# Attention blocks on one core: values products on raw fp32, and the block output built with tokens on partitions

## What is computed

```python
xn  = layernorm(x)
# attention branch on xn (it normalizes again)
uv  = silu(layernorm(xn, ln_w, ln_b) @ uv_w.T + uv_b)        # 640 wide
u, v, base = uv[..., :256], uv[..., 256:512], uv[..., 512:]
q, k = rope(base * gamma + beta)
kernel = square(relu(q @ k.T / sqrt(128) + bias))            # 512 x 512 per block
attn = (u * (kernel @ v)) @ o_w.T + o_b + xn
# feed-forward branch on xn
ffn  = squared_relu(xn @ W_sh_up) @ W_sh_down                # shared expert
ffn += sum over the 2 chosen of 8 experts: weight * squared_relu(xn @ W_up[e]) @ W_down[e]
out  = x + attn + ffn
```

## Time and profile before

| what | value |
|---|---|
| runs | 454.51, 454.58, 455.42 us; median 454.58 us |
| the profiled execution, its own time | 456.13 us |
| its span, first to last instruction | 454.3 us |
| mean granted TensorE clock over the span | 0.927 of full |
| busy share of the span | PE 82%, PEld 66%, DVE 65%, ACT 54%, POOL 39% |
| preparation | 0 to 73.9 us |
| turns, from the first rotate_sum to the last mix | 73.9 to 270.3 us |
| expert stage and collection | 271.4 to 454.3 us |

### The profile page before, as it was taken

The page is one execution under the profiler, slowest core; times in us unless marked ns, Lnnn a source line. Parts: engine busy times, 40 slices in busy tenths (PEclk is TensorE's granted clock), DMA queues, the critical chain, the costliest instruction groups (busy, mean ns, idle before and its releaser), DMA issues.

```text
span 454.3 us, 8228 instructions
## 1 busy us (share of the span) xinstructions
PE 371.5 (82%) x2041; PEld 299.2 (66%) x2042; DVE 294.0 (65%) x726; ACT 245.2 (54%) x453; POOL 176.2 (39%) x159
## 2 busy tenths in 40 slices
PE   1168457799998989899999969999999999999800
PEld 1157435566665667566756638999999999999700
DVE  2889798988988888989899822333333333333245
ACT  0203027565676766665656715666666666666400
POOL 0486004562534526180716200444444444444500
PEclk9995567999999999999999997999999999999955
DMA  8618993000000001010100101221222212212089
GB/s 227 212 46 237 231 191 61 29 30 19 23 23 18 29 6 41 0 47 0 41 6 30 42 0 30 66 63 60 64 59 63 64 57 65 64 57 65 36 251 309
DMA packets 49792, 33.65 MB, mean 74 GB/s; under 512 B 5747, under 2 KB 46195, under 8 KB 49780
## 3 DMA queue, kind: packets, MB, share of 16 engines
q1 hardware_dynamic: 29120, 16.27, 12.8%
q10 hardware_dynamic: 16308, 8.26, 9.1%
q0 software_dynamic: 4352, 8.99, 5.5%
HBM read 17.63 MB, written 15.87 MB: 74 GB/s over the span
## 4 chain that ended last, share of the span: by engine, by line
PE 50%; DVE 21%; issue 12%; ACT 6%; ACTq 4%; DMA 4%; DVEq 2%; POOL 0%; POOLq 0%
PE bank L1133 14%; PE bank L1114 7%; PE bank L908 7%; PE bank L909 6%; PE bank L910 6%; DVE work L748 3%; PE bank L1020 3%; ACT base_qk L414 3%; DVE xs L613 3%; ACTq L356 2%; PE bank L946 2%; PE bank L1107 2%; DMA work<-results 2%; DVE qk_lo L725 2%; DVE k_lo L757 2%
## 5 line engine op out<-in xcount | busy, mean ns | idle before, releaser
L865 POOL DMA_INDIRECT slots_in<-xs,slot_now x64 | 75.2, 1176 | 124.5 <-DVE xs L634 77.9
L895 POOL DMA_INDIRECT results<-work x72 | 69.2, 960 | 109.2 <-DVE work L822 107.4
L822 DVE TENSOR_SCALAR work<-bank,work 128x128 f32<-128x128 f32 x72 | 25.2, 350 | 93.5 <-PE bank L1133 93.5
L1133 PEld LDWEIGHTS bank<-wdn,work 128*128 128x128 f32 x576 | 75.1, 191 | 6.0
L1133 PE MATMUL bank<-wdn,work 128*128 x576 | 75.7, 274 | 0.0
L499 ACT ACTIVATE work<-bank 128x512 f32<-128x512 f32 x72 | 43.1, 599 | 14.7 <-PE bank L1114 14.7
L505 ACT ACTIVATE work<-bank 128x512 f32<-128x512 f32 x72 | 43.1, 598 | 8.9 <-PE bank L910 3.4
L1114 PE MATMUL bank<-cst,work 128*128 128x128 f32 x288 | 43.9, 276 | 0.0
L908 PE MATMUL bank<-wup_lo,x_hi 128*128 x72 | 35.3, 491 | 1.0 <-DVE x_lo L813 1.0
L493 ACT CAST x_hi<-bank 128x128 fp32r<-128x128 f32 x72 | 19.0, 266 | 30.8 <-PE bank L1107 30.8
L1114 PEld LDWEIGHTS bank<-cst,work 128*128 128x128 f32 x288 | 34.2, 143 | 0.5 <-issue 0.4
(11 more groups left out here) (177 smaller groups left out, 824.1 us busy)
## 6 DMA issues: line engine op xcount, KB each, us to landing
slots_in<-spare ACTq DMA_DIRECT2D x1, 4680.0 KB, 31.7
work<-slots_in SPq DMA_DIRECT2D x36, 130.0 KB, 2.2
x_all<-in_L_attn_x SPq DMA_DIRECT2D x4, 512.0 KB, 8.7
work<-in_L_ffn_W_up SPq DMA_DIRECT2D x4, 512.0 KB, 3.5
wdn<-in_L_ffn_W_down SPq DMA_DIRECT2D x4, 512.0 KB, 7.3
work<-results SPq DMA_DIRECT2D x8, 256.0 KB, 7.2
work<-results ACTq DMA_DIRECT2D x8, 256.0 KB, 7.7
out<-x_all SPq DMA_DIRECT2D x8, 256.0 KB, 5.7
```

The costliest lines, as they stand in the source:

```text
L865: pool.indirect_dma_start(slots_in, bass.IndirectOffsetOnAxis(slot_now[:, k, t:t + 1], 0), xs1[:, k, t, :], None).then_inc(tokens_sent, 16)
L895: pool.indirect_dma_start(results, bass.IndirectOffsetOnAxis(dest[:, at:at + 1], 0), slot_y[:, k, :], None).then_inc(returned[k], 16)
L1133: last = pe.matmul(P_Y[h][:, 0:D], hid_t[:, h, rows], wdn[:, of, c, :].rearrange("p a d -> p (a d)"), start=(c == 0), stop=(c == HC - 1))
```

## The change

- values: v and kern stay in plain fp32 (v is 128x4x256, kern 128x4x512, all four key tiles at once). No v_split, no kernel_hi, no kernel_lo, one silu of v in place of two. Each `product` of three matmuls becomes one plain fp32 matmul.
- output: the sums in P_OUT have tokens on partitions. The stationary operand is a 128-column slice of sh or g, the moving one shdn or ow with 128 columns; each old matmul becomes four. output_out and output_turned are gone, and mix reads P_OUT. The bias o_b comes in as the first product of the bank: a constant 1/64 stationary (`halves`) times `ob_pair`, which holds o_b rounded to fp32r on 64 partitions and the remainder on the other 64. Two VectorE operations of the preparation build `ob_pair`; o_b is now loaded as a broadcast row.
- order: on TensorE the output of the block before moves behind shared_up 3, shared_down 0 and 1 move behind the base parts, the x1 rows behind values 2. On VectorE mix moves ahead of second_rows_lo. sh has four buffers.

```diff
 act.  def v_silu(b):
-                    act.activation(v_hi[:, 2 * n:2 * n + 2, :]..., part, ACT.Silu)
-                    act.activation(part, part, ACT.Silu).then_inc(v_hi_made, 1)
+                    act.activation(v[:, 2 * n:2 * n + 2, :]..., part, ACT.Silu).then_inc(v_made, 1)
 act.  def turn(b, first, last):
...
-                if not first:
-                    output_out(b - 1)
-                kernel_hi(b, 0)
-                kernel_hi(b, 1)
...
-                kernel_hi(b, 2)
-                kernel_hi(b, 3)
 dve.  preparation, between lnb_bc and uvw_hi
+            dve.memset(halves[:, :].bitcast(F32), 1.0 / HALF)
+            link(prep_chain, dve.tensor_copy(ob_pair[:, :, :], ob_bc[:, :].unsqueeze(1).broadcast_to([P, TB, D])))
+            dve.tensor_tensor(ob_pair[HALF:S], ob_bc[HALF:S, :].unsqueeze(1).broadcast_to([HALF, TB, D]),
+                              ob_pair[HALF:S].bitcast(F32), ALU.subtract).then_inc(ob_made, 1)
 dve.  def turn(b, first, last):
                 kernel_square(b, 0)
                 kernel_square(b, 1)
-                v_split(b)
                 if not last:
                     second_norm(b + 1)
-                kernel_lo(b, 0)
-                kernel_lo(b, 1)
                 kernel_square(b, 2)
                 kernel_square(b, 3)
+                if not first:
+                    mix(b - 1)
                 if not last:
                     second_rows_lo(b + 1)
                     first_norm(b + 1)
-                if not first:
-                    mix(b - 1)
-                kernel_lo(b, 2)
-                kernel_lo(b, 3)
 dve.  def mix(b):
-                dve.wait_ge(out_turned, START + b + 1)
+                dve.wait_ge(out_acc, START + b + 1)
...
-                dve.tensor_tensor(rows, P_FIN[:, :]..., rows, ALU.add).then_inc(mixed, 1)
+                dve.tensor_tensor(rows, P_OUT[:, :]..., rows, ALU.add).then_inc(mixed, 1)
 pe.
+            def output_bias(b):
+                pe.wait_ge(mixed, START + b)
+                pe.matmul(P_OUT[:, :], halves[:, :], ob_pair[:, :, :].rearrange("p t d -> p (t d)"), start=True, stop=False)
+
             def shared_down(b, c):
                 pe.wait_ge(sh_made, START + b * HC + (c + 1))
-                pe.matmul(P_OUT[:, :], shdn[:, c, :], sh[:, c % 2, :], start=(c == 0), stop=False).then_inc(shdn_done, 1)
+                for t in range(TB):
+                    rows = slice(t * P, (t + 1) * P)
+                    last = pe.matmul(P_OUT[:, rows], sh[:, c, rows], shdn[:, c, :], start=False, stop=False)
+                last.then_inc(shdn_done, 1)
...
             def values(b, j):
-                pe.wait_ge(k_lo_made, b * TB + (j + 1))
+                pe.wait_ge(kern_made, b * TB + (j + 1))
...
-                    last = product(P_AV[e][:, :], v_hi[:, j, e * P:(e + 1) * P], v_lo[:, j, e * P:(e + 1) * P],
-                                   k_hi[:, j % 2, :], k_lo[:, j % 2, :], start=(j == 0), stop=(j == TB - 1))
+                    last = pe.matmul(P_AV[e][:, :], v[:, j, e * P:(e + 1) * P], kern[:, j, :], start=(j == 0), stop=(j == TB - 1))
...
             def output(b):
...
-                    last = pe.matmul(P_OUT[:, :], ow[:, e * D:(e + 1) * D], g[:, e, :], start=False, stop=(e == 1))
+                    for t in range(TB):
+                        rows = slice(t * P, (t + 1) * P)
+                        last = pe.matmul(P_OUT[:, rows], g[:, e, rows], ow[:, e * D:(e + 1) * D], start=False, stop=(e == 1 and t == TB - 1))
 pe.   def turn(b, first, last):
                 scores(b, 0)
                 scores(b, 1)
-                if not first:
-                    output(b - 1)
                 scores(b, 2)
                 scores(b, 3)
                 shared_up(b, 2)
                 shared_up(b, 3)
-                pe.wait_ge(out_t_made, START + b)
-                shared_down(b, 0)
-                shared_down(b, 1)
                 if not first:
-                    output_turned(b - 1)
+                    output(b - 1)
                 values(b, 0)
                 if not last:
                     second_rows_turned(b + 1)
                 values(b, 1)
                 if not last:
                     base_part(b + 1)
+                output_bias(b)
+                shared_down(b, 0)
+                shared_down(b, 1)
+                values(b, 2)
+                if not last:
                     first_rows_turned(b + 1)
-                values(b, 2)
                 values(b, 3)
                 shared_down(b, 2)
                 shared_down(b, 3)
```

More of the change, by code:

```diff
@@ L99, in build @@
         x1_hi, x1_lo = sb("x1_hi", [P, T], F32R), sb("x1_lo", [P, T], F32R)
-        v_hi, v_lo = sb("v_hi", [P, TB, EU], F32R), sb("v_lo", [P, TB, EU], F32R)
+        v = sb("v", [P, TB, EU])
         qk_hi, qk_lo = sb("qk_hi", [P, 2, T], F32R), sb("qk_lo", [P, 2, T], F32R)
-        k_hi, k_lo = sb("k_hi", [P, 2, T], F32R), sb("k_lo", [P, 2, T], F32R)
         g = sb("g", [P, 2, T])
+        kern = sb("kern", [P, TB, T])
         cos_sin = sb("cos_sin", [P, 2, T])
@@ L138, in build @@
         rot1, rot2 = cut(3072, (2, T)), cut(4096, (2, T))
-        kern = cut(5120, (2, T))
-        sh = cut(6144, (2, T))
-        out_t = cut(7168, (T,))
         slot_x = cut(0, (2, 2, ROW_W))
@@ L154, in build @@
         inv1, var2, inv2 = sb("inv1", [P, NT]), sb("var2", [P, NT]), sb("inv2", [P, NT])
-        lnw_c, lnb_c, ob_c = sb("lnw_c", [P, 1]), sb("lnb_c", [P, 1]), sb("ob_c", [P, 1])
+        lnw_c, lnb_c = sb("lnw_c", [P, 1]), sb("lnb_c", [P, 1])
+        ob_bc, ob_pair = sb("ob_bc", [P, D]), sb("ob_pair", [P, TB, D], F32R)
+        halves = sb("halves", [P, P], F32R)
+        sh = sb("sh", [P, HC, T])
         uvb_c, uvbias = sb("uvb_c", [P, 4]), sb("uvbias", [P, 4])
@@ L350, in _ @@
         def _(act):
-            for s in (base_made, out_t_made, sh_relu, sh_made, silu_b_made, ut_made):
+            for s in (base_made, sh_relu, sh_made, silu_b_made, ut_made, v_made):
                 act.sem_inc(s, START)
@@ L432, in shared_relu @@
                 product = of_ring(f"sh{c}", b)
-                act.wait_ge(shdn_done, START + b * HC + (c - 1) if c >= 2 else START + b * HC)
-                act.activation(sh[:, c % 2, :], product, ACT.Relu).then_inc(sh_relu, 1)
+                act.wait_ge(shdn_done, START + b * HC)
+                act.activation(sh[:, c, :], product, ACT.Relu).then_inc(sh_relu, 1)
             def shared_square(b, c):
                 act.wait_ge(sh_relu, START + b * HC + (c + 1))
-                act.activation(sh[:, c % 2, :], sh[:, c % 2, :], ACT.Square).then_inc(sh_made, 1)
-            def kernel_hi(b, j):
-                act.wait_ge(kern_made, b * TB + (j + 1))
-                act.wait_ge(av_done, START + b * TB + (j - 1) if j >= 2 else START + b * TB)
-                act.copy(k_hi[:, j % 2, :], kern[:, j % 2, :]).then_inc(k_hi_made, 1)
-            def output_out(b):
-                act.wait_ge(out_acc, START + b + 1)
-                act.wait_ge(out_turned, START + b)
-                act.activation(out_t, P_OUT[:, :], ACT.Identity, bias=ob_c[:, :]).then_inc(out_t_made, 1)
+                act.activation(sh[:, c, :], sh[:, c, :], ACT.Square).then_inc(sh_made, 1)
             def turn(b, first, last):
@@ L482, in _ @@
             sequence_turns(act, turn)
-            output_out(B - 1)
             act.wait_ge(mixed, START + B)
@@ L516, in _ @@
         def _(dve):
-            for s in (rx_copied, qk_made, qk_lo_made, mixed, g_made, kern_biased, x2_lo_made, x1_lo_made, v_biased, v_lo_made, rot2_made):
+            for s in (rx_copied, qk_made, qk_lo_made, mixed, g_made, kern_biased, x2_lo_made, x1_lo_made, v_biased, rot2_made):
                 dve.sem_inc(s, START)
@@ L732, in v_bias @@
                                       vb_bc[:, :].unsqueeze(1).broadcast_to([P, 2, EU]), ALU.add).then_inc(v_biased, 1)
[L734 to L740 removed]
             def kernel_square(b, j):
                 dve.wait_ge(ring_ready, START + b * NRING + (RING.index(f"qk{j}") + 1))
[L745 to L746 removed]
+                if j == 0:
+                    dve.wait_ge(av_done, START + b * TB)
                 at = (TB - 1 - j) * P
[L748 removed]
+                dve.scalar_tensor_tensor(kern[:, j, :], ring(f"qk{j}")[:, :], float(S) ** -0.5,
                                          bias_t[:, at:at + T], ALU.mult, ALU.add).then_inc(kern_biased, 1)
                 dve.wait_ge(kern_biased, START + b * TB + (j + 1))
[L751 removed]
+                dve.scalar_tensor_tensor(kern[:, j, :], kern[:, j, :], 0.0, kern[:, j, :],
                                          ALU.max, ALU.mult).then_inc(kern_made, 1)
[L754 to L758 removed]
             def gate(b):
@@ L902, in _ @@
         def _(pe):
-            for s in (logits_made, rx_turned, shdn_done, av_done, out_acc, out_turned, ring_ready):
+            for s in (logits_made, rx_turned, shdn_done, av_done, out_acc, ring_ready):
                 pe.sem_inc(s, START)
@@ L959, in _ @@
```

(2 more changed lines are left out.)

49 lines of the change are left out of this document (12 added, 37 removed).

## The result

The changed kernel took 471.44 us (median of 472.19, 470.69, 473.5 and 466.0) against 454.58: ratio 1.033, interval 1.024 to 1.042, slower. The ratio is that of the means without 473.5, which lies more than 1.5% above the fastest run of its kernel; all later ratios are made so. The prediction was 443.5 with a range of 440.5 to 449.5. The same file was run again later, unedited, in two other sessions, and took 443.32 us (ratio 0.976, 0.969 to 0.984) and 444.56 us (0.978, 0.971 to 0.984).

What follows compares the result with a forecast made beforehand. VectorE was taken as the bound, TensorE 2.4 us a turn behind. Terms -8.2 - 3.9 + 1.5 - 1.2 + 0.7 = -11.1 us from the profiled 456.13 gave 445.0, or 443.5 against the median; range 440.5 to 449.5.

Steps and rivals of the forecast that it cites:

- Does anything stop TensorE?: Step checking TensorE's handovers through a turn; found four slacks of 0.2 to 0.9 us and a turn of 23.3 us.
- The slower rival: Shared_down and output: loads of 128-column records show, 3.8 us more a turn, 472.7 us in all; chance 0.06.
- the rule of the Trainium skill that the prediction set against its rows: Shared_down and output: loads overlap only for another row group, so 48 records pay 107 ns each, a turn 28.3 us.
- Preparation +0.7: Preparation: two ob_pair operations on VectorE delay uvw_lo by some 1.2 us, partly absorbed; +0.7 us, bounds 0 and 1.4.
- Turn 0, -3.9: First turn, without output: gate comes at 19.3 us in place of 23.25, so -3.9 us.
- Six inner turns, 23.3 each and -8.2: Inner turns: TensorE becomes the bound at 23.3 us a turn in place of 24.67, -8.2 us over six.
- The sum of 23.2: TensorE's work in an inner turn: 22.2 + 1.05 + 0.15 - 0.48 + 0.24 = 23.2 us.
- the 0.1 for add_rows: Inner turns: GpSimd's add_rows stretches a VectorE square, taken as 0.1 us a turn, bound 1.0.
- Last turn +1.5: Last turn, gate to gate: all TensorE at 21.1 us in place of 19.6, +1.5 us.
- Tail -1.2: From the last gate to mix's end: 4.3 us in place of 5.5, as output_out and transposes go, -1.2 us.
- a new wait on TensorE: Rival in the turns: late add_rows or x2_lo takes most of the gain, 24.1 us a turn, 449.1 us; chance 0.17.
- Its SBUF sentence: Squares beside add_rows: by the skill's rule a square that starts first loses nothing, by the rows 1.47 us.

Runs made afterwards that it cites:

- g1: The changed kernel itself, unedited, run again on chip D: 443.32 us, ratio 0.976.
- h1: The changed kernel itself, unedited, run again on chip C: 444.56 us, ratio 0.978.
- f1: The changed kernel with GpSimd's sends of a turn started only when v_bias has read v0: 441.63 us, ratio 0.970.

## Why the prediction was right and wrong

**Against the recorded result it was wrong by 28 us, on the other side.** The step that failed is "Does anything stop TensorE?". It counted each handover from the end of the record, as the trace of before lets one do (0.01 us to the increment), and gave v_part, shared_up and u0 no slack of their own: v_bias was taken as always in time. In the recorded session the word of v0 came 4 us late, and the list of four slacks had no entry for it. The fast session's rows give that slack: v_bias has freed u0's bank at 122.50, and u0 starts at 123.65, 1.15 us later. A v_bias 3.92 us late leaves 2.77, and TensorE stands 2.75. The slower rival came out near the number (472.7 for 471.4) and is wrong all the same: it priced loads that show in the 128-column records, and these run at 0.111 us each in both sessions (sixteen records in 1.95 us, the last one modelled 0.28). By the rule of the Trainium skill that the prediction set against its rows ("TensorE: Matmul & The Clock Gate"; it stands in section "The mechanism", one heading above the one that the prediction names) they would pay a load each; both traces of after disagree with it, as that of before did. The same section also lets a load for the background weight buffer go ahead of running matmuls, and that would fit these rows.

**Against the kernel where its signals come in time it was right, 443.3 and 444.6 for 443.5, and by errors that cancel, so part of it is luck.** By its own steps, from the trace of g1 (span 440.5):

- Preparation +0.7: rotate_sum of turn 0 starts at 74.55 against 73.89, +0.66. Right.
- Turn 0, -3.9: measured 96.45 - 74.55 = 21.90 against 23.25, -1.35. Wrong by 2.5, and by 4.2 in h1, where the turn takes 23.59. I let first_norm alone wait for add_rows in turn 0. The rows show add_rows on the squares, and TensorE, which has no output in this turn, already there:
```profile
83.62 2.31 DVE L726 SCALAR_TENSOR_TENSOR kern<-kern 128x512 f32<-128x512 f32 x1
84.19 1.19 POOL L836 TENSOR_TENSOR x_all<-x_all,xs 128x512 f32<-128x512 f32 x1
85.85 0.68 DVE L723 SCALAR_TENSOR_TENSOR kern<-bank,bias_t 128x512 f32<-128x512 f32 x1
86.68 0.63 PE L941 MATMUL bank<-cst,xs 128*128 128x128 f32 x4 [2.35 <-DVE kern L723]
```
 f1 moves add_rows to 88.08, behind the squares, and TensorE's stop falls to 0.75 us:
```profile
83.83 0.69 DVE L726 SCALAR_TENSOR_TENSOR kern<-kern 128x512 f32<-128x512 f32 x1
84.44 0.68 DVE L723 SCALAR_TENSOR_TENSOR kern<-bank,bias_t 128x512 f32<-128x512 f32 x1
85.27 0.63 PE L942 MATMUL bank<-cst,xs 128*128 128x128 f32 x4 [0.75 <-DVE kern L723]
```
 Its turn 0 takes 20.55, 1.35 less than g1's and 3.0 less than h1's; its inner turns are the same 137.75. In h1 the stop is the same (2.27 against 2.35 us), but TensorE comes back at the lower clock level, 0.50 of full granted from 87 to 90 us, where g1 has 1.00. That is where f1's 1 to 3 us come from, and not from late signals. **f1 has the lowest medians of the study, 441.5 to 442.4 us on two chips**, though its interval and the changed kernel's overlap on both.
- Six inner turns, 23.3 each and -8.2: measured 22.96 and -10.3. TensorE is the bound, as said, and with no stop at all. The sum of 23.2 was 0.24 too high, about the size of the doubt named there (switches between kinds of products counted twice), and the 0.1 for add_rows was not needed: with the sends ending at 125.1, add_rows falls into VectorE's wait for the scores.
- Last turn +1.5: 20.69 against 19.59, +1.1. Tail -1.2: gate at 254.89, mix ends at 259.10, 4.21 against 5.50, -1.3.
- Sum from the start to mix's end: +0.66 - 1.35 - 10.3 + 1.1 - 1.3 = -11.2 against -11.1. In h1 it is -9.0.
- Behind that the prediction put nothing, and the spans differ by more: 454.3 - 440.5 = 13.8. From mix's end to the experts' first down product it takes 9.35 us before, 6.49 in g1 and 7.92 in h1, and from there to the last one 149.7 to 149.8 in all three. The granted clock in the 3 us ahead of that first product is 0.66, 1.00 and 0.71 of full: the way into the expert stage gave another 2.9 and 1.4 us that no term stood for.

What should have shown it did: gate starts at 119.42, 0.15 us behind values 3 (last record 118.68, 0.59 long; expected within 0.1), with VectorE idle for 0.51 ahead of it, values records at 0.43, output records at 0.111. The rival "a new wait on TensorE" was right in kind for turn 0 alone. Its SBUF sentence bears out once more: square 2 began 0.57 us ahead of add_rows and still took 2.31 in place of 0.69. By the rule of the Trainium skill ("SBUF — State Buffer", section "SBUF: two separate sides") it would have kept the port as the first to start. What the prediction left out: each such square began while a send was already running on GpSimd (here from 83.20 to 84.16). A send alone doesn't stretch one, as f1's at 83.83 shows, 0.53 us into a send and 0.69 long. GpSimd's starts are rough in the profile, so this counts against the rule without settling it.

## What to carry to other kernels

A wait that a profile puts down to "remote" or "an unknown queue" in a kernel on one core was no wait for data here: compare the end of the record with the arrival of its signal before anything in the code is blamed. When variants fall into two groups, look first whether the groups are also two chips; so the unedited kernel should run beside its variants each time. Here that would have saved most of the runs. A kernel before that keeps its time on all chips (454.4 to 455.6 us) doesn't tell them apart. In a turn without its usual work (the first one), an engine reaches each handover earlier, and slacks taken from the inner turns do not hold.

## What the runs showed of the hardware

- TensorE's increments can arrive late behind the record that carries them, in order, while the products behind them run on: in the recorded run's looped turns 1.3 to 4.8 us for shared_down, and v0's, v1's, sh0's and sh1's then all within 0.2 us. It came only beside GpSimd's indirect transfers and only in some sessions; the price was 27.2 us in six turns. The recorded run has late increments of up to 1.7 us beside the experts' indirect transfers too (most from 406 to 421 us), where the stage lost nothing: 149.7 us from the first down product to the last, as elsewhere.
- Behind five of six stops of 2.70 to 2.85 us TensorE came back at the lower clock level: the next records took 0.80 and 0.63 us in place of 0.39. TensorE's longer busy time is 10.4 us of the 27.2. Behind one of 2.70 (100.5 to 103.2 us) it did not, and behind turn 0's stop it did in h1 (2.27 us) and not in g1 (2.35 us).
- An indirect transfer of GpSimd can be stretched by VectorE too: 1.97 us in place of 0.96 where it started 0.08 us behind the 1,024-column qk_lo (123.16). The one at 120.64, 0.02 us behind a rotate_sum of as many columns, took 0.96.
